# A two-layer graph network: the second layer's scalar products computed from a stored, turned x

## The reference

```
msg  = (scalars and vectors of x[dst]) times (edge attributes) times small weights
a    = segment_sum(msg, src)                      # a0: 64 scalars, a1: 32 vectors
u0   = einsum('nu,nv,uvw->nw', x0, a0, W_ss) + einsum('nui,nvi,uvw->nw', x1, a1, W_vv) + x0 @ L_s
u1   = einsum('nu,nvi,uvw->nwi', x0, a1, W_sv) + einsum('nui,nv,uvw->nwi', x1, a0, W_vs) + x1 @ L_v
x    = layernorm(x + x + u)
```

## Time and profile before

| | us |
|---|---|
| median of 3 runs | 6800.21 (6799.34 to 6801.61) |
| the profiled execution | 6798.1 |
| its span, first to last instruction | 6796.4 |
| PE busy | 5635.1 (83%) |
| DVE busy | 5464.6 (80%) |
| POOL busy | 5269.3 (78%) |
| ACT busy | 3740.8 (55%) |
| 16 DMA engines | 203 GB/s mean |

### The profile page before, as it was taken

One profiled execution on the slowest core, in us unless ns is written; L12 is line 12 of the kernel. 1 busy time (PEld: TensorE's weight loads), 2 busy tenths in 40 slices (PEclk: granted clock), 3 DMA queues, 4 the chain that ended last, 5 costly groups with the idle time before them and its releaser, 6 DMA issues.

```text
span 6796.4 us, 145388 instructions
## 1 busy us (share of the span) xinstructions
PE 5635.1 (83%) x52295; PEld 4584.6 (67%) x52295; DVE 5464.6 (80%) x7299; ACT 3740.8 (55%) x11578; POOL 5269.3 (78%) x4099
## 2 busy tenths in 40 slices
PE   5566666666664799999999999999589999999998
PEld 3444545555553677777777777777468777777877
DVE  6777777777775788888888888888379988988998
ACT  2333333333332566666666666666267777777776
POOL 2777777777777478888888888888778888788887
PEclk7878878788787999999999999999799999999999
DMA  7888888888884387878787878787422222222222
GB/s 223 268 256 256 262 258 261 259 255 258 261 259 140 123 261 257 264 257 265 255 265 254 266 255 263 251 268 254 143 88 92 93 99 95 92 94 100 92 93 74
DMA packets 681148, 1380.99 MB, mean 203 GB/s; under 512 B 106047, under 2 KB 487661, under 8 KB 654447
## 3 DMA queue, kind: packets, MB, share of 16 engines
q1 hardware_dynamic: 527695, 1090.23, 51.0%
q0 software_dynamic: 152736, 281.45, 12.2%
HBM read 587.20 MB, written 784.08 MB: 202 GB/s over the span
## 4 chain that ended last, share of the span: by engine, by line
PE 43%; POOL 14%; SPq 11%; DVE 10%; DMA 9%; issue 8%; ACT 6%; POOLq 0%; DVEq 0%; ACTq 0%
POOL slots L647 11%; PE node_ps L1352 8%; PE prods_ps L1301 8%; DMA rec<-edge_recs 5%; DVE zs L1034 4%; PE prods_ps L1304 3%; PE prods_ps L1320 3%; POOL q L704 3%; SPq L372 3%; PE node_ps L1369 3%; DMA slots<-pay,slot_all 3%; SPq L346 3%; PE m_ps L1369 2%; PE turn_ps L1339 2%; ACT onehot L1701 2%
## 5 line engine op out<-in xcount | busy, mean ns | idle before, releaser
L647 POOL DMA_INDIRECT slots<-pay,slot_all x3136 | 3261.0, 1040 | 1017.5 <-issue 792.1
L1701 ACT ACTIVATE onehot<-node_iota,msgs 128x125 f32<-128x125 f32 x3400 | 1030.2, 397 | 122.4 <-POOLq L691 122.4
L1352 PEld LDWEIGHTS node_ps<-msgs,onehot 128*125 128x125 f32 x6800 | 932.0, 188 | 139.2 <-issue 98.5
L1352 PE MATMUL node_ps<-msgs,onehot 128*125 128x160 f32 x6800 | 980.7, 303 | 35.8 <-ACT onehot L1707 25.2
L1084 DVE TENSOR_REDUCE upd<-work 125x48 f32<-125x3072 f32 x300 | 1003.9, 3346 | 6.9
L1071 DVE TENSOR_TENSOR work<-prods_ps,yv 125x1024 f32<-125x1024 f32 x800 | 931.0, 1216 | 64.3 <-PE prods_ps L1305 63.4
L1217 PE MATMUL m_ps<-win,picks_sb 125*128 125x160 f32 x3136 | 666.1, 341 | 274.7 <-ACT pay L1502 266.5
L731 POOL TENSOR_TENSOR q<-xt,yv 125x3072 f32<-125x3072 f32 x100 | 547.6, 5476 | 339.7 <-PE turn_ps L1339 322.6
L1217 PEld LDWEIGHTS m_ps<-win,picks_sb 125*128 125x128 f32 x3136 | 527.8, 218 | 359.1 <-issue 263.6
L1487 ACT COPY picks_sb<-s_ps 125x512 f32<-125x512 f32 x392 | 229.4, 585 | 710.7 <-PE s_ps L1199 603.7
L1034 DVE TENSOR_TENSOR zs<-prods_ps,x_t 128x1000 f32<-128x1000 f32 x400 | 469.5, 1195 | 134.3 <-PE prods_ps L1302 134.3
(11 more groups left out here) (273 smaller groups left out, 13501.3 us busy)
## 6 DMA issues: line engine op xcount, KB each, us to landing
msgs<-slots SPq DMA_DIRECT2D x200, 1428.0 KB, 6.4
slots<-zero SPq DMA_DIRECT2D x183, 1386.0 KB
win<-table SPq DMA_DIRECT2D x784, 160.0 KB
picks<-picks_sb SPq DMA_DIRECT2D x196, 512.0 KB
picks_sb<-picks SPq DMA_DIRECT2D x196, 512.0 KB
table<-tab SPq DMA_DIRECT2D x200, 350.0 KB
slots<-pay,slot_all POOLq DMA_INDIRECT x3136
spill_in<-spill_sums SPq DMA_DIRECT2D x200, 80.0 KB, 6.1
```

Source lines behind the costliest of these rows:

```text
L647: g.indirect_dma_start(out=slots[layer][:, :], out_offset=bass.IndirectOffsetOnAxis(ap=slot_all[:, j:j + 1], axis=0), in_=pay[q][:, j - UB ...
L1352: te.matmul(node_ps[0:HM, 0:D], onehot[:, j, :], msgs[b][:, j, 0:D], start=(j == 0), stop=False)
L1701: last = ac.activation(onehot[:, j, :], node_iota[:, :], ACT.Square, bias=msgs[b][:, j, LOCAL:LOCAL + 1], scale=-1.0)
```

## The change

In the second layer the scalar term is computed in the other order. For a tile, x is needed as 64 rows (u) by 125 nodes, each row spread over 64 partitions (v). The first layer already turns its result to build the second layer's message table; that turned tile (`ts_t`, now in two buffers) is also stored to a new DRAM tensor `xt_mid` (`store_turned_x`). In the second layer SP loads, for each tile, the 64 rows with each spread over 64 partitions: u = 0 to 31 on partitions 0 to 63, u = 32 to 63 on the others (`load_spread_x`, two DMAs into `xb`). VectorE multiplies these by a in place, in four pieces. PE sums over v and u with 32 matmuls of 128 rows onto 64 columns, alternating between the two halves of the output partitions (`spread_sums`, in two parts), and the vector part goes into the same place (`vector_sums`, with weights and data changed over). `linear_last` adds both halves. The weights W_ss of this layer are laid out to suit. The rounds r = 0 to 3 of `bilinear` and `scalar_sums` are gone from the second layer. One of the buffers `xb` lies over `zs`, the other over the second layer's message windows and payloads.

```diff
+        xb = [zs[:, :, :, :, :].rearrange("p r h q n -> p (r h q) n"),
+              late[:, 0:SPAN * HM].rearrange("p (j n) -> p j n", n=HM)]
...
+            def load_spread_x(k):
+                t, half, b = k
+                for z in range(2):
+                    sp.dma_start(xb[b][S * z:S * z + S, :, :].rearrange("p j n -> p (j n)"),
+                                 xt_mid[t, SPAN * z:SPAN * z + SPAN, :].rearrange("j n -> (j n)").unsqueeze(0).broadcast_to([S, SPAN * HM])
+                                 ).then_inc(xb_in[b], 16)
+            def store_turned_x(k):
+                m, mh, b = k
+                sp.wait_ge(LS[1]["t_turn_out"], m + 1)
+                sp.dma_start(xt_mid[m, :, :], ts_t[b][:, :]).then_inc(xt_put[b], 16)
...
+                    if layer == 1:
+                        if r == 0:
+                            ve.wait_ge(s["y_turned_out"], 3 * n + 1)
+                            ve.wait_ge(xb_in[nb], xb_first + 32 * nh + 32)
+                        j0 = SPAN // PIECES_Z * r
+                        z = xb[nb][:, j0:j0 + SPAN // PIECES_Z, :]
+                        ve.tensor_tensor(z, z, a2_t[nb][:, :].unsqueeze(1).broadcast_to([P, SPAN // PIECES_Z, HM]), ALU.mult).then_inc(s["prods_used"], 1)
+                        return
...
+                def spread_sums(part):
+                    if not nodes:
+                        return
+                    if part == 0 and within(n, 1, NT):
+                        te.wait_ge(s["h_ready"], n)
+                    to, half_j = m_ps[:, 256:256 + HM], SPAN // 2
+                    wz = w.bil[:, 0:SS // 2].rearrange("p (j c) -> p j c", c=S)
+                    for j in range(half_j * part, half_j * (part + 1)):
+                        if j % (SPAN // PIECES_Z) == 0:
+                            te.wait_ge(s["prods_used"], USES[1] * n + j // (SPAN // PIECES_Z) + 1)
+                        side = S * (j % 2)
+                        te.matmul(to[side:side + S, :], wz[:, j, :], xb[nb][:, j, :], start=(j < 2), stop=False, tile_position=(0, side))
+                def vector_sums():
...
+                    for j in range(QC):
+                        side = S * (j % 2)
+                        mm = te.matmul(to[side:side + S, :], w.vv[:, j, :], q_t[:, j, :], start=False, stop=(j >= QC - 2), tile_position=(0, side))
+                    mm.then_inc(s["prods"], 1)
...
+                    te.wait_ge(s["ss_out"], n + 1)
+                    te.matmul(m_ps[0:HM, S:D], v_t[nb][:, :], w.lin_u[:, :], start=True, stop=True)
+                    te.matmul(m_ps[0:HM, 0:S], x2_t[nb][:, :], w.lin0[:, :], start=True, stop=False)
+                    te.matmul(m_ps[0:HM, 0:S], ss_t[:, :], both_halves[:, :], start=False, stop=True).then_inc(s["lin"], 1)
...
-                    for r in range(SUMS):
-                        bilinear(r)
+                    if nodes:
+                        for r in range(R0, SUMS):
+                            bilinear(r)
                     sum_edges()
                     turn_q(0)
-                    scalar_sums()
+                    spread_sums(0)
                     turn_q(1)
+                    spread_sums(1)
+                    vector_sums()
                     turn_y()
-                    linear()
+                    linear_last()
```

More of the change, by code:

```diff
@@ L63 @@
 BAND = 4 * R0 - 2
+SPAN = S // 2
+PIECES_Z = 4
 Y_OUT = 3
@@ L426, in load_node_weights @@
                     sp.dma_start(t.lin1[r, r], w["lu_v"]).then_inc(w_in, 16)
[L427 to L430, removed]
+                if layer == 0:
+                    ss_halves = w["u_ss"].rearrange("v (r h c) -> h v r c", h=2, c=512)
+                    ss_rows = t.bil[:, 0:SS // 2].rearrange("p (r c) -> p r c", c=512)
+                    ss = ((ss_rows[0:S], ss_halves[0]), (ss_rows[S:P], ss_halves[1]))
+                else:
+                    ss = tuple((t.bil[S * z:S * z + S, 0:SS // 2], w["u_ss"][S * z:S * z + S, :]) for z in range(2))
+                for to, frm in (*ss, (t.bil[0:S, SS // 2:].rearrange("p (w k) -> p w k", k=V), w["u_sv"]),
                                 (t.bil[S:P, SS // 2:].rearrange("p (w k) -> p w k", k=V), w["u_vs"]),
@@ L1100, in node_step @@
                 if nodes and layer == 1:
-                    for r in range(R0):
+                    for r in range(PIECES_Z):
                         scalars(r)
@@ L1286, in bilinear @@
                         return
-                    if r == 0:
+                    if layer == 1:
                         te.wait_ge(s["y_turned_out"], 3 * n + 3)
-                    if r >= 2:
+                        if within(n, 1, NT):
+                            te.wait_ge(s["prods_used"], USES[1] * (n - 1) + used(1, r))
+                            te.wait_ge(s["copied"], R1 * (n - 1) + r - R0 + 1)
+                    elif r == 0:
+                        te.wait_ge(s["y_turned_out"], 3 * n + 3)
+                    if layer == 1:
+                        pass
+                    elif r >= 2:
                         te.wait_ge(s["prods_used"], USES[layer] * n + used(layer, r - 2))
@@ L1358, in linear @@
                     te.wait_ge(s["q_turned_out"], 2 * n + 2)
-                    if layer == 0 and edges:
+                    if edges:
                         te.wait_ge(s["y_out"], Y_OUT * t + Y_OUT)
-                    if layer == 1 and within(n, 1, NT):
-                        te.wait_ge(s["h_ready"], n)
-                    to = (node_ps, m_ps)[layer]
-                    if layer == 0:
-                        te.matmul(to[0:HM, 0:D], ident2[0:HM, 0:HM], xt[nb][0:HM, :], start=True, stop=False)
-                    te.matmul(to[0:HM, S:D], v_t[nb][:, :], w.lin_u[:, :], start=layer == 1, stop=layer == 1)
-                    te.matmul(to[0:HM, 0:S], x2_t[nb][:, :], w.lin0[:, :], start=layer == 1, stop=False)
+                    to = node_ps
+                    te.matmul(to[0:HM, 0:D], ident2[0:HM, 0:HM], xt[nb][0:HM, :], start=True, stop=False)
+                    te.matmul(to[0:HM, S:D], v_t[nb][:, :], w.lin_u[:, :], start=False, stop=False)
+                    te.matmul(to[0:HM, 0:S], x2_t[nb][:, :], w.lin0[:, :], start=False, stop=False)
                     for j in range(QC):
@@ L1458, in table_turned @@
                     ac.wait_ge(s["t_mm"], m)
-                ac.copy(ts_t[:, :], turn_ps[0:S, 0:HM])
+                if layer == 1 and within(m, 2, NT):
+                    ac.wait_ge(xt_put[b], xt_first + 16 * mh)
+                ac.copy(ts_t[b][:, :], turn_ps[0:S, 0:HM])
                 ac.copy(tv_t[:, :], turn_ps[0:3 * V, HM:2 * HM]).then_inc(s["t_turn_out"], 1)
@@ L1731, with laid_out @@
 }
-def laid_out(name, a):
+def laid_out(name, a, layer):
+    if name == "u_ss" and layer == 1:
+        return np.ascontiguousarray(a.reshape(2, SPAN, S, S).transpose(0, 2, 1, 3).reshape(P, SS // 2))
     if name in ("u_ss", "u_vs"):
```

52 lines of the change are left out of this document (33 added, 19 removed).

## The result

The changed kernel took 7144.79 us (median of 4 runs, 7140.29 to 7147.33), the kernel before 6800.91 us beside it (6799.34 to 6809.21). The ratio is 1.0502, 95% interval 1.0484 to 1.0521: slower by about 341 us, where the prediction had 278 (7079 us). The first layer shows nothing: from 2400 to 4600 us PE is busy for 2105.89 us where it was for 2105.52. The loss is in the second layer's 99 periods. From the first message sums to the last they take 21.65 us in the mean, where they took 18.28: 3.36 x 99 = 333 us. The two profiled spans differ by 349 us; of the other 16, 10 come after the last sums (45.2 us instead of 35.1) and 6 lie ahead of the first layer's sums.

What follows compares the result with a forecast made beforehand. PE's chain bound the second layer at 18.30 us a tile; the one-hot ring would replace it at 19.07. 6798.1 + 76 (ring) + 203 (clock) = 7077, with 2.1 more 7079 us; own range 7030 to 7150, 8-in-10 range 6870 to 7330.

Steps and rivals of the forecast that it cites:

- the ring: Second layer: message sums, then ScalarE's one-hot work, sharing one buffer; predicted to grow from 16.44 to 19.07 us, +76 us.
- the clock: PE's clock falls after idling before each tile's message sums in the second layer: 2.05 us a tile, +203 us.
- signs of a wrong forecast: Second layer: PE waiting for VectorE's multiplies, the one-hot work waiting for messages, or PE staying the chain.
- the chain: Second layer: the chain of waits through PE that set the old 18.30 us period; predicted new length 14.5 us.
- 32 rounds at 0.115 and 8 more: PE, second layer: spread sums in 32 two-record rounds, 3.68 us, and the vector part in 8, 0.92 us.
- the third and fourth rivals: PE's column halves run one after the other, 7535 us, 7%; or cheap rounds keep the ring under 18.30, 6650, 7%.
- PE stands for 4.6 us: PE's predicted idle time before the message sums in every second-layer tile: 19.07 less its own 14.5 us.
- The first rival: Second layer: same longer ring, but PE's clock stays at 1.00: 6876 us, chance 9%.
- The loads cost nothing: 9.0 us for 2000 KB: Second layer's spread x loads take 9.0 us a tile, hidden by slack: 0 us added.
- the second rival: Second layer's spread load becomes the bound, from some 13.5 us a load: 7305 us at 17 us; chance 13%.
- The slack of 4 to 5 us: Second layer: predicted margin between the messages landing and the one-hot work that reads them, 4 to 5 us.
- I count 0: VectorE's four second-layer multiplies, reading SBUF on both sides instead of PSUM: 0; 0.5 us if POOL cost 10%.

Runs made afterwards that it cites:

- kernel 6: Changed kernel plus six unread matmuls in PE's gap before the message sums, and VectorE's multiplies reading their second operand from PSUM: 6895.2 us, ratio 1.0132.
- kernel 4: Changed kernel without the spread loads of x; the multiplies read resident weights instead and no longer write in place: 7138.4 us, ratio 1.0489.
- kernel 8: Changed kernel with y turned after the first spread half, one-hot squares started earlier, and the multiplies' second operand from PSUM: 7147.8 us, ratio 1.0502.
- kernel 10: As kernel 9, but the multiplies read both operands from SBUF as in the changed kernel: 7031.6 us, ratio 1.0336.
- kernel 1: Changed kernel with only the second operand of VectorE's four multiplies read from PSUM instead of SBUF: 7086.0 us, ratio 1.0413.
- kernel 9: As kernel 8, with the next tile's messages issued ahead of x, the spread loads and the wait for h: 6684.3 us, ratio 0.9825.

## Why the prediction was right, and what it mis-sized

The direction and the mechanism held, with the ring and the clock for 281 of the 341 us, and none of what it named as signs of a wrong forecast is there: PE doesn't wait for the multiplies, the one-hot work doesn't wait for messages, and PE is no longer the chain. By its own steps:

- *PE gets 32 rounds at 0.115 and 8 more: 3.68 + 0.92 us.* In PE's rows of the changed kernel 3.63 and 0.96. Two column halves do work side by side; the third and fourth rivals fell by this.
- *The ring becomes 19.07 us, +76.* 14.02 from the sums' end to the one-hot end and 5.21 of sums make 19.23 in kernel 6; +90 by its ratio.
- *PE stands for 4.6 us and the clock falls in each tile, 2.05 us, +203.* It stands 5.35 us in most tiles and up to 7.9, and the clock costs 191 us. The first rival, where the clock holds, exists only as kernel 6, where PE was kept busy: 6895 against the 6876 given for it.
- *The loads cost nothing: 9.0 us for 2000 KB.* Right for this kernel (kernel 4: 0.0013, no more than the interval). The size was about right too, but in part by luck, as these rows do not move as fast as the messages. Two windows of the changed kernel, in which only spread rows and then only messages were under way, columns as above:

```profile
6014.00:6021.00 7.00, 5.96 (x22) 5.96 (x23) 7.00 (x3) 4.91 (x12) 6.22 (x3) 0.53 1.06 219
6023.00:6026.00 3.00, 3.00 (x42) 2.53 (x40) 3.00 (x3) 0.98 (x3) 0.00 (x0) 1.00 0.91 371
```

At 219 GB/s a load takes 9.3 us, under the 13.5 from which the second rival would have counted. The 9.0 came from the messages' 6.4 us to landing, of which only 3.9 are moving at 371 GB/s. The slack of 4 to 5 us was gone as soon as the one-hot work came earlier and h later (kernel 8).
- *VectorE's four multiplies: "I count 0"; at worst "0.5 us on an engine with over 2 us to spare".* This is the term that was mis-sized. They cost 1.2 us more each in the mean, 4.9 us a tile, and filled VectorE to 97%: 61 us here. With the ring's 14 us too few and the clock's 12 too many, that is nearly all of the 63 us that the forecast lacked. That the 14 and the 12 cancel is luck, and so is that 7145 still lies in the forecast's own range: its upper end, 7150, came from the clock and the rounds alone.

That step rested on the mean of one group, 1216 ns for an add of two SBUF operands. All 138 of these stood beside POOL's indirect DMAs, and none beside an elementwise instruction of POOL's. The trace of the kernel before had the other case too, in 7 tiles between 2404 and 2559 us, ahead of the stretch of that group. VectorE's timeline of the kernel before, there:

```profile
2430.20 2.40 DVE L1056 TENSOR_TENSOR q<-q 125x1024 f32<-125x1024 f32 x1
```

POOL's timeline of the kernel before, beside it:

```profile
2429.45 0.96 POOL L647 DMA_INDIRECT slots<-pay,slot_all  x1 [0.30 <-issue]
2430.44 1.08 POOL L704 TENSOR_TENSOR q<-xt,yv 125x512 f32<-125x512 f32 x1
```

2.40 us in place of 1.2, with POOL's 1.08 us multiply beside it. In the second layer POOL computes 81% of the time, so this was the row to price the change by.

The Trainium skill, "SBUF — State Buffer", section "SBUF: two separate sides", says that VectorE and GpSimd have one pair of ports in common, that a VectorE instruction with two SBUF inputs takes it against a GpSimd one that reads SBUF, and that whichever comes second stands until the first is through. The runs agree: 3.35 = 1.19 + 2.16 us beside POOL's instructions of 2.4, both engines longer, and neither with one operand in PSUM; one multiply of kernel 10 beside POOL's outer product of 5.5 us took 6.46. On who comes second the row at 2430.20 doesn't agree: by the profile VectorE's add starts 0.24 us before POOL's multiply, and it is the add that is held up. The prediction left the rule out, and by it the multiplies would have had a price.

## What to carry to other kernels

Where an operand moves from PSUM to SBUF, look what POOL does in the stretch where the instruction will run, and take the price from an instance with that neighbour, not from a group's mean in another stage. Sparing PE work was worth nothing here until the next rings were opened too: the one-hot ring (19.23 us in kernel 6), the messages' place in SyncE's queue (kernel 8) and VectorE's multiplies (kernel 10) each kept the kernel slower than before, and only with all three eased was it 1.8% faster. A cost that is hidden is not small: the multiplies were worth 61, 148 or 348 us by what else stood in the way.

## What the runs showed of the hardware

- VectorE's multiply with two SBUF operands and POOL's elementwise instructions take turns: 1.19 us alone, 3.35 us between two of POOL's; POOL's add 2.75 us in the mean instead of 2.36. Beside POOL's indirect DMAs an add of VectorE's with two SBUF operands took 1.22 us (138 of 138), and with one operand in PSUM the multiply took 1.19 us beside POOL's adds and outer product (kernel 1).
- PE's clock fell in each of 99 tiles after gaps of 5.0 to 7.9 us (changed kernel), and with two gaps of 1.07 and 1.94 us a tile in about one tile of seven (kernel 9).
- The rows of x, each spread over 64 partitions, moved at 219 GB/s, the messages right behind them at 371 (changed kernel).
